# TensorE's instruction stream: a register loop over 24 of 32 samples, or every sample written out

## The reference, cut to what matters

```
x = x + conv(x, w0, 9 taps, 4 groups) + ctx0(cond) + bias
x = x + (sum_k att1[k] * W1[k]) @ x + att1 @ bias1      # 1x1 convolution whose weights depend on the sample
x = x + (sum_k att2[k] * W2[k]) @ x + att2 @ bias2
x = x + conv(x, w3, 9 taps, 4 groups) + ctx3(cond) + bias
```

## Time and profile before

| | |
|---|---|
| median of 3 runs | 675.41 us (675.36 to 676.52) |
| the profiled execution's own time | 675.46 us |
| its span, first to last instruction | 673.7 us |
| PE busy | 651.5 us (97%), 11,200 matmuls |
| DVE, ACT, POOL busy | 510.7, 262.8, 243.1 us |
| mean granted clock of TensorE | 0.995 of full speed |
| instruction fetches on queue q8 | 28 packets, 0.46 MB |

### The profile page before, as it was taken

One profiled execution on the slowest core, in us unless ns is written; L12 is line 12 of the kernel. 1 busy time (PEld: TensorE's weight loads), 2 busy tenths in 40 slices (PEclk: granted clock), 3 DMA queues, 4 the chain that ended last, 5 costly groups with the idle time before them and its releaser, 6 DMA issues.

```text
span 673.7 us, 24614 instructions
## 1 busy us (share of the span) xinstructions
PE 651.5 (97%) x11200; PEld 630.1 (94%) x11200; DVE 510.7 (76%) x945; ACT 262.8 (39%) x323; POOL 243.1 (36%) x91
## 2 busy tenths in 40 slices
PE   4989999999999999999999999999999999999994
PEld 3679888999999999999999999999999999999994
DVE  5699778788778777777877777787877787788736
ACT  5432443333443343343334234334324433433435
POOL 5022432324443333444243344334244433334220
PEclk9999999999999999999999999999999999999998
DMA  7137888998888899888889888889988888987646
GB/s 234 69 101 159 196 192 176 176 180 184 197 194 192 153 210 163 195 198 195 186 154 218 158 194 196 192 167 183 186 180 198 191 191 152 212 158 145 132 105 157
DMA packets 50181, 118.24 MB, mean 176 GB/s; under 512 B 5541, under 2 KB 26074, under 8 KB 42330
## 3 DMA queue, kind: packets, MB, share of 16 engines
q1 hardware_dynamic: 49586, 116.95, 81.0%
q10 hardware_dynamic: 360, 0.69, 0.5%
q0 software_dynamic: 192, 0.02, 0.0%
HBM read 35.33 MB, written 33.55 MB: 102 GB/s over the span
## 4 chain that ended last, share of the span: by engine, by line
PE 94%; DVE 2%; DMA 2%; ACT 1%; issue 1%; ACTq 0%; SPq 0%; DVEq 0%
PE ps L829 79%; PE ps L896 13%; DMA out_planes<-out_taps 1%; DMA out_sb<-in_L_cond_weight 1%; PE ps L883 1%; ACT out_sb L537 1%; DVE x_lo L598 1%; DVE y_lo L606 0%; ACT x_hi L559 0%; PE ps L929 0%; DVE acc L645 0%; DVE mat L645 0%; PE ps L922 0%; ACT out_taps L485 0%; PE ps L995 0%
## 5 line engine op out<-in xcount | busy, mean ns | idle before, releaser
L399 POOL COPY out_sb<-out_planes 128x2048 f32<-128x2048 f32 x30 | 117.4, 3915 | 283.3 <-DMA out_planes<-out_taps 283.3
L467 ACT ACTIVATE y_hi<-ps,bias_tab 128x512 fp32r<-128x512 f32 x128 | 77.5, 689 | 188.9 <-PE ps L829 185.0
L393 POOL COPY x_planes<-x_in 128x2048 f32<-128x2048 f32 x29 | 113.0, 3896 | 90.5 <-DVE x_lo L598 90.5
L616 DVE SCALAR_TENSOR_TENSOR z_lo<-ps,bias_tab,z_hi 128x1024 fp32r<-128x1024 f32 x62 | 76.7, 1279 | 59.7 <-ACT z_hi L477 59.7
L606 DVE SCALAR_TENSOR_TENSOR y_lo<-ps,bias_tab,y_hi 128x512 fp32r<-128x512 f32 x128 | 87.3, 746 | 38.7 <-ACT y_hi L467 38.6
L829 PE MATMUL ps<-z_hi,taps_lo 32*128 32x512 f32 x1488 | 104.2, 398 | 1.0 <-issue 1.0
L829 PE MATMUL ps<-x_hi,taps_hi 32*128 32x512 f32 x1536 | 103.2, 399 | 1.0 <-ACT x_hi L559 0.7
L829 PE MATMUL ps<-x_hi,taps_lo 32*128 32x512 f32 x1536 | 101.3, 392 | 0.0
L829 PE MATMUL ps<-x_lo,taps_hi 32*128 32x512 f32 x1536 | 100.5, 390 | 0.0
L896 PE MATMUL ps<-y_hi,mix_w 32*128 32x512 f32 x1024 | 99.3, 390 | 0.9 <-DVE y_lo L606 0.9
L829 PE MATMUL ps<-z_lo,taps_hi 32*128 32x512 f32 x1488 | 97.7, 390 | 0.1
(11 more groups left out here) (118 smaller groups left out, 619.2 us busy)
## 6 DMA issues: line engine op xcount, KB each, us to landing
x_in<-in_x SPq DMA_DIRECT2D x31, 1024.0 KB, 11.5
out_planes<-out_taps SPq DMA_DIRECT2D x122, 256.0 KB, 8.5
out<-out_sb SPq DMA_DIRECT2D x30, 1024.0 KB, 4.2
mix_w<-prod SPq DMA_DIRECT2D x128, 128.0 KB, 4.6
x_in<-in_x SPq DMA_DIRECT2D x2, 512.0 KB, 5.0
out<-x_planes SPq DMA_DIRECT2D x8, 128.0 KB, 2.2
out_taps<-in_L_cond_weight SPq DMA_DIRECT2D x1, 512.0 KB, 5.1
mix_w<-in_L_cond_weight SPq DMA_DIRECT2D x1, 512.0 KB, 6.4
```

Source lines behind the costliest of these rows:

```text
L393: pool.tensor_copy(x_planes[:, :, :], planes(x_in[t.par(d)], slice(0, S))).then_inc(x_planed, 1)
L399: pool.tensor_copy(out_sb[t.par(d)][:, :].rearrange("c (s p) -> c p s", p=PH), out_planes[:, :, :])\
L467: act.activation(y_hi[:, g, :], ps[:, bank(t, 0) + g, :], ACT.Identity, bias=bias_tab[:, b, g:g + 1]).then_inc(y_hi_done, 1)
L616: dve.scalar_tensor_tensor(out=z_home(t, 0)[1][:, 2 * h:2 * h + 2, 1:S + 1], in0=ps[:, k:k + 2, :], scalar=bias_tab[:, b, 2 * G:BIAS], in1 ...
```

## The change

The bounds of the loop, `LOOP`, are removed. TensorE's program calls `one(t)` for each of the samples 1 to 31 with whole numbers. The work, its order, the semaphores waited for and the values they are compared with stay the same; the values become constants in samples 4 to 27. The other engines' programs are not touched.

```diff
-        LOOP = (2, (N - 4) // 2)
-
         ALL = [Step(i // 2, i % 2) for i in range(N + 1)]
...
             pe.wait_ge(taps_lo_done[1], PH)
-            for t in ALL[1:2 * LOOP[0]]:
-                one(t)
-            with pe.Fori(LOOP[0], LOOP[1]) as half:
-                one(Step(half, 0))
-                one(Step(half, 1))
-            for t in ALL[2 * LOOP[1]:N]:
+            for t in ALL[1:N]:
                 one(t)
```

## The result

The written-out program takes 685.5 us (median of 4 runs, 683.81 to 686.17) beside 675.56 us: a ratio of 1.0142, interval 1.0130 to 1.0154. The forecast was 683.5 us, in a range of 677.0 to 691.5. The profiled execution took 685.42 us, 683.6 of it span.

The account below looks back on a forecast made before the run. TensorE's instruction stream was taken to bound the kernel (PE has work for 97% of the span). 675.46 us + 0 for what is removed + 8 for late fetches = 683.5 us, range 677.0 to 691.5 us.

Parts of the forecast that it names:

- What the change removes: TensorE's loop: twelve branches and the body's register instructions, worth 0 us on the path (-0.5 to +0.5 us).
- The number of fetches: TensorE's code queue q8: 87 packets instead of 28, 59 more, all in samples 6 to 27.
- What a fetch costs: TensorE's code fetches: mostly in time, but one requested just behind relays and x load is late by up to about 3 us.
- turn-taking rule: DMA engines alternate between queues packet by packet, so a fetch waits one packet, not a burst: added cost about 0.
- The size: Late fetches in samples 6 to 27: about 8 us in all, with 1 and 15 us as ends.
- phase count: Packet boundaries against a 3 us place per sample: one hit per three samples, 1.2 us each, 7 to 8 hits, 8 to 10 us.
- second-order term: Data DMAs shifted by fetches may delay VectorE's evacuation, which conv0 waits for: 0 to 1 us, taken as 0.
- Hidden: Rival: TensorE's fetches all stay hidden, 675.5 us (675.0 to 676.2); chance 0.08.
- Faster: Rival: shifted packet boundaries all stay clear of the burst and sample 5's gap goes, 674.2 us; chance 0.05.
- Many late: Case: many of TensorE's fetches in the written-out samples are late, above 691 us; chance 0.07.

Follow-up runs that it names:

- late load: x load issued only when the four relay DMAs have landed: 673.29 us in the written-out kernel, 673.21 us in the kernel with the loop.
- cut loads: x loads from sample 2 on cut to the first 64 of 2,048 columns: 673.34 us in the kernel with the loop, 673.85 us written out.
- shifted loop: Kernel with the loop, 32 tiny matmuls added at the head of TensorE's program, moving later code half a packet: 678.84 us, ratio 1.0042.
- body of four: Kernel with the loop, each pass holding four samples (six passes), 2,764 instructions instead of 1,400: 715.32 us, ratio 1.0513.

## Why the prediction was right, point by point

**What the change removes** was 0, as forecast: undisturbed samples take 19.77 to 19.81 us in both kernels, and in the version with the late load the loop and the written-out code are 0.08 us apart.

**The number of fetches** was right: 87 packets, 59 more.

**What a fetch costs** was right in its mechanism: a request that falls behind the relays and the x load waits until they have nearly drained. Shown by taking the load away (10 us become 0.5), by moving it (0.1), and by moving the code (gaps leave the instruction and keep the packet grid). When a packet is asked for no profile shows; that is inferred from its start. The turn-taking rule of the Trainium skill, "DMA: Bandwidth & Descriptors", section "Queues, rings and completion order", which the prediction set against it, would have given 0; whatever the engines do between queues, a code packet started 9 us behind a load's issue here.

**The size** was near by luck in part. Seven fetch gaps in samples 6 to 27 (7 to 8 expected) cost some 7.2 us: their samples are 8.6 us longer, and most of the other 1.4 us is VectorE's in three of them. The mean is 1.0 us a hit, not the 1.2 us of the sum, and the largest 1.6 us and not 3. The phase count behind the 8 us doesn't carry it. Worked through with its own figures, a place 3 us wide among boundaries 2.5 us apart takes 1.2 boundaries in three samples, each late by 1.5 us on average: 22 / 3 x 1.2 x 1.5 = 13 us. With the width that the largest gap suggests, 1.6 us, it would be 4.7 hits of 0.8 us, 3.8 us. Both are estimates; the hits came more often than the second and were smaller than in the first.

**The second-order term was mis-sized**: it was held at 0 (0 to 1 us) and came to about 3 us (1.4 + 0.8 + 0.5 in samples 13 and 20, and the 0.4 us of the undisturbed ones). Sample 13 has no fetch gap and is 0.82 us longer. The chain there: start, us, what.

```profile
295.44 0.70 DVE prod_sum L651
296.14 0.02 issue
296.16 2.58 DVE prod L654
298.75 0.02 issue
298.77 0.29 DVE prod L656
299.06 0.43 DVE x_lo L596
299.50 1.68 issue
301.18 1.41 DVE out_taps L624 x2
302.60 0.14 issue
302.73 12.87 PE ps L827 x215
```

`conv0` waits for the evacuation, that for `x_lo`, that for the product's cast, and the cast of 128 x 128 takes 2.58 us. (The "issue" of 1.68 us is the rest of `x_lo`, which takes 2.29 us in VectorE's timeline.) The group of all casts, after, and in the two versions with the late load (written out, looped): count, busy us, mean ns.

```profile
L654 DVE CAST prod<-prod_sum 128x128 fp32r<-128x128 f32 x32 | 53.4, 1670 | 1.5 <-ACT prod_sum L543 0.4
```

```profile
L656 DVE CAST prod<-prod_sum 128x128 fp32r<-128x128 f32 x32 | 34.3, 1073 | 1.5 <-ACT prod_sum L545 0.4
```

```profile
L658 DVE CAST prod<-prod_sum 128x128 fp32r<-128x128 f32 x32 | 15.7, 489 | 1.6 <-ACT prod_sum L547 0.6
```

Before, the mean was 1.28 us. In these profiles a cast lasts 0.23 us where it has no overlap with GpSimd's weaving copy, and where it overlaps for 0.2 us or more, 0.08 us more than that overlap, up to 2.6 us: it hardly moves while that copy runs. TensorE's gaps move VectorE's work against the weaving, and the fetched packets sit among the relays that the weaving waits for. The two versions with the late load have no gap between 140 and 600 us and differ in the packets alone: there the cast's mean is 1.07 us with 87 of them and 0.49 us with 28. With the cut loads it is the other way round, 0.90 and 1.01 us. So packets alone can lengthen the overlap and needn't; how the 12 us of the written-out kernel divide between packets and gaps stays open.

**The rivals.** "Hidden" fell with the seven gaps. "Faster" fell too, and the shifted loop shows why such luck isn't to be counted on. "Many late" didn't come: seven samples of 22 had a fetch gap.

## What to carry to other kernels

When a program that keeps one engine full is unrolled, its code has to be streamed in during the run, and as here a packet may start late behind a burst of data: look for the code queue in the trace, for idle time without a releaser, and count the instructions between two such gaps. If the count is a multiple of a packet, look for the cure in the order and size of the data bursts ahead of the fetch; one wait on SP was enough here. The loop helped only while its whole body stayed resident. And before a transfer is moved to a quieter place, ask what is queued next there.

## What the runs showed of the hardware that was not expected

- Between a code packet's end and TensorE's next instruction lie 1.3 to 1.6 us, in the fetch gaps of the written-out profile.
- A body of 1,400 instructions ran eleven more passes without a packet, one of 2,764 was fetched again in each pass; a branch back to code that had to be brought in cost 3.2 us and more.
- The written-out kernel's gaps (1.6 us beyond the pace of the matmuls at most) left TensorE's granted clock at 1.00; behind the first two gaps at the branch of the body of four (3.2 and 3.8 us) it was 0.64 and 0.50 for 4 to 5 us.
- A 128 x 128 cast on VectorE took 0.23 us alone and up to 2.6 us beside a 3.9 us GpSimd copy.
- With the late load the five runs of the looped kernel lay within 0.7 us (672.64 to 673.31) where the kernel before spread over 3.1 us beside it (eleven runs). With that few runs the link to the burst is a guess.
